# Expert stages on sorted rows: from two groups of batches with closed 128-row pieces to chunks whose pieces stay open

## The chip, the cores and the metric

The kernel runs on one core of one Trainium2 chip. The metric is the device time of one launch in microseconds (us). The engines are TensorE (PE; its weight loads are listed as PEld), VectorE (DVE), ScalarE (ACT), GpSimd (POOL) and SyncE (SP), which only issues transfers. Each has its own list of instructions, run in order; they meet through semaphores.

## The reference, cut to what matters

```python
x = x + attn_a(layernorm(x))      # linear attention, rope, elu+1 features, 16 heads of 8
x = x + ffn(layernorm(x))         # stage 1 of the experts
x = x + attn_b(layernorm(x))      # causal "log" attention with two score passes
x = x + ffn(layernorm(x))         # stage 2, the same weights

def ffn(x):                       # x is (8*512, 128); I = 256, E = 8, TOP_K = 2
    shared = silu(x @ sg_w.T) * (x @ su_w.T) @ sd_w.T
    probs = sigmoid(x @ router_w.T + routing_bias)
    topk_p, topk_idx = top_k(probs, 2); topk_p = topk_p / topk_p.sum(-1)
    # every row: two experts, each down(silu(gate x) * up x), weighted and added
    return shared + routed
```

There are 8 batches of 512 rows of 128 floats, so 4096 rows and 8192 pairs of a row and an expert.

## The kernel before, in words

All rows stay on the core (`x_res`, four tiles of 128 rows a batch). The four parts of the network run one after the other, each with its own program on each engine, and each part already does some work of the next one ("lead").

**Linear attention** goes batch by batch (`a_tensor_step`, `a_vector_step`, ...: steps 1 to 9, step 9 only ends batch 8).

**An expert stage** (class `Experts`) first normalises and transposes each batch and computes router logits. Then it *routes* a group of batches: a chain of small DVE instructions, each of which waits for the one before through `chain`, finds the two experts of each row (`vector_first`, `vector_second`), PE counts ranks (`tensor_ranks`), and DVE makes of them a row number in a list sorted by expert (`vector_place`, rows_of) and the expert of each 128-row slot (`vector_table`, table). POOL then *sends* every tile twice with an indirect DMA into `x_sorted` in DRAM (`send_tiles`, line 950; two per 128 rows), padded so that every expert's rows fill whole slots of 128. SP loads the slots four at a time (a *quad*, 1027), PE transposes them (743), and two slots make a *pair*: gate and up (`pair_gate_up`, 758, with the weights of the slot's expert), silu on ACT (863), the product on DVE (1204), a transpose (771), ACT's copy (871), down (`pair_down`, 781). ACT evicts and stores a quad to `y_sorted` (885, 890). When the quads of a group are stored, POOL *fetches* each batch's 8 tiles with indirect DMAs (960), and DVE adds them to `x_res` with their gates (`add_routed`, 1220). The *shared* expert is dense, batch by batch, and stands between pairs where the table `shared_after` says (724, 735, DVE 1195 and 1211).

Before, stage 1 has groups of 3 and 5 batches: 31 + 47 slots, 16 + 24 pairs. Stage 2 has 6 and 2: 55 + 23 slots, 28 + 12 pairs. Each group is padded by itself, so a stage is 40 pairs. Group 0 of stage 1 is routed and sent in step 7 of the linear attention; group 0 of stage 2 is routed during the last steps of the log attention (`lead_vector(k)`; k counts steps after the first score pass has ended) and sent from k = 13 on, three tiles a step, the rest behind it (`lead_pool`, `pool`). The group behind is routed while pairs of the first run. In the last 12 pairs of stage 1 the log attention's start stands in the slots of `TENSOR_LEAD`, `SCALAR_LEAD` and `VECTOR_LEAD` (projections of its first batch: q, ky, k).

**Log attention** (610 us): 80 steps of two score passes, B 16 steps behind A. POOL fetches the rows of stage 1's last batches during it, one tile a step (`late_fetch`).

## Time and profile before

| | us |
|---|---|
| median of 3 runs | 1392.99 (1386.32 to 1395.81) |
| the profiled execution | 1393.95 |
| its span | 1392.2 |
| mean granted TensorE clock | 0.831 |
| linear attention, to the first pair | 0 to 172.9 |
| stage 1 | 172.9 to about 449 |
| log attention, to the first pair of stage 2 | about 449 to 1129.8 |
| stage 2 | 1129.8 to 1392.2 |

The span runs from the first to the last instruction of one execution; 1.75 us of the profiled execution's time lie around it. The times at which parts begin and end are start times of their first and last matmuls, and neighbouring parts overlap on the other engines.

### The profile page before, as it was taken

What the parts mean: (1) busy time and instruction counts of PE and PEld (TensorE: products, weight loads), DVE (VectorE), ACT (ScalarE), POOL (GpSimd) and SP (SyncE); (2) the same over time, 40 slices, a digit from 0 to 9 for tenths busy, and PEclk for the clock granted to TensorE, in tenths of its full rate; (3) what the DMA queues carried; (4) which work ended last, traced back from release to release, by engine and by line L of the source; (5) the groups of instructions that cost most, each with busy time, mean ns of one, the idle gap of its engine ahead of it and who ended that gap; (6) DMA issues with size and microseconds to landing.
All of it is one profiled execution on the core that took longest, in us unless ns stands there. A gap on an engine that the chain in (4) does not pass through costs nothing.

```text
span 1392.2 us, 19740 instructions
## 1 busy us (share of the span) xinstructions
PE 957.8 (69%) x6976; PEld 569.3 (41%) x6976; DVE 657.1 (47%) x1314; ACT 607.2 (44%) x876; POOL 457.9 (33%) x527
## 2 busy tenths in 40 slices
PE   4776388528588766878787878786756078799241
PEld 3665256426355323333333333333333056566120
DVE  4787234202132345786777777775363033222022
ACT  1231063103145564777686877766422034254020
POOL 1113410640610343554433333342117600401734
PEclk9787589769889677999898999996587599999665
DMA  9400210121224344344443434311001211122222
GB/s 304 144 1 19 62 32 16 48 68 37 72 69 141 127 151 151 130 150 140 142 142 123 142 125 156 116 44 55 31 1 46 67 31 31 61 74 83 60 66 81
DMA packets 110557, 123.29 MB, mean 89 GB/s; under 512 B 9472, under 2 KB 72832, under 8 KB 110336
## 3 DMA queue, kind: packets, MB, share of 16 engines
q1 hardware_dynamic: 81664, 95.01, 20.9%
q0 software_dynamic: 8192, 16.79, 4.1%
q10 hardware_dynamic: 20608, 10.23, 2.5%
q8 instruction: 61, 1.00, 0.3%
q14 instruction: 32, 0.26, 0.1%
HBM read 60.52 MB, written 61.47 MB: 88 GB/s over the span
## 4 chain that ended last, share of the span: by engine, by line
PE 40%; DVE 16%; another core or an unknown queue 15%; issue 10%; DMA 9%; ACT 5%; SPq 4%; POOL 1%; DVEq 0%; POOLq 0%; ACTq 0%
PE psum L758 8%; DVE ring_b L1675 7%; PE psum L1470 5%; PE psum L1422 5%; PE psum L781 4%; DMA stacks<-stack_qr 4%; PE psum L724 2%; PE psum L771 2%; SPq L1820 2%; PE psum L735 2%; PE psum L1487 2%; DMA stacks<-stack_ky 2%; SPq L1815 2%; PE psum L743 1%
## 5 line engine op out<-in xcount | busy, mean ns | idle before, releaser
L1675 DVE TENSOR_SCALAR ring_b<-psum 128x1024 int32<-128x1024 int32 x160 | 195.7, 1223 | 129.0 <-PE psum L1422 128.8
L1549 ACT ACTIVATE ring_a<-psum 128x1024 f32<-128x1024 f32 x160 | 163.5, 1026 | 140.9 <-PE psum L1422 139.3
L1422 PE MATMUL psum<-stacks 32*128 32x128 f32 (+3 forms) x1024 | 107.1, 399 | 129.8 <-DVE ring_b L1675 97.2
L1555 ACT ACTIVATE ring_b<-ring_b 128x1024 f32<-128x1024 f32 x160 | 168.6, 1055 | 44.3 <-DVE ring_b L1675 44.3
L960 POOL DMA_INDIRECT r_rows<-y_sorted,rows_of x128 | 128.3, 1002 | 180.7 <-DMA y_sorted<-y_out 133.9
L758 PE MATMUL psum<-w_expert,ring_a 128*128 x312 | 160.8, 640 | 32.5 <-ACT ring_a L878 27.7
L950 POOL DMA_INDIRECT x_sorted<-r_rows,rows_of x128 | 124.1, 970 | 157.8 <-DVE rows_of L1170 120.5
L1781 POOL TENSOR_SCALAR_AFFINE_SELECT ring_b<-ring_b 128x512 f32<-128x512 f32 (+1 forms) x112 | 81.6, 741 | 284.5 <-ACT ring_b L1555 284.5
L1204 DVE TENSOR_TENSOR ring_b<-psum,ring_b 128x512 f32<-128x512 f32 x80 | 54.2, 677 | 223.9 <-ACT ring_b L863 184.9
L1422 PEld LDWEIGHTS psum<-stacks 32*128 32x128 f32 x1024 | 62.9, 201 | 225.0 <-ACT ring_a L1549 84.8
L1667 DVE TENSOR_SCALAR ring_a<-ring_a 128x1024 f32<-128x1024 f32 x160 | 122.7, 770 | 34.4 <-ACT ring_a L1549 34.4
L781 PE MATMUL psum<-w_expert,ring_b 128*128 x624 | 92.4, 295 | 47.2 <-DVE x_res L1211 24.6
L863 ACT ACTIVATE ring_b<-psum 128x512 f32<-128x512 f32 x80 | 47.0, 588 | 173.1 <-PE psum L758 106.8
L1470 PE MATMUL psum<-ring_b,values 128*32 128x256 f32 (+3 forms) x1024 | 111.7, 513 | 0.0
L1470 PE MATMUL psum<-ring_b,ones_s 128*32 128x256 f32 (+3 forms) x1024 | 110.1, 506 | 0.0
L1781 POOL TENSOR_SCALAR_AFFINE_SELECT ring_a<-ring_a 128x512 f32<-128x512 f32 (+1 forms) x112 | 83.7, 761 | 75.6 <-DVE ring_a L1667 75.6
L781 PEld LDWEIGHTS psum<-w_expert,ring_b 128*128 128x128 f32 x624 | 84.4, 210 | 49.1 <-issue 49.1
L1454 PE MATMUL psum<-ring_a,ones_s 128*32 128x256 f32 (+3 forms) x1024 | 93.9, 476 | 2.5 <-POOL ring_a L1781 1.7
L735 PE MATMUL psum<-w_expert,ring_b 128*128 128x128 f32 x256 | 37.9, 309 | 78.4 <-DVE ring_b L1195 60.9
L758 PEld LDWEIGHTS psum<-w_expert,ring_a 128*128 128x128 f32 x312 | 57.6, 205 | 78.0 <-issue 77.8
L735 PEld LDWEIGHTS psum<-w_expert,ring_b 128*128 128x128 f32 x256 | 34.7, 217 | 85.4 <-DVE ring_b L1195 66.5
L771 PEld LDWEIGHTS psum<-identity,ring_b 128*128 128x128 f32 x312 | 40.8, 148 | 68.0 <-issue 65.9
(175 smaller groups left out, 1291.5 us busy)
## 6 DMA issues: line engine op xcount, KB each, us to landing
ring_a<-x_sorted SPq DMA_DIRECT2D x36, 256.0 KB
y_sorted<-y_out ACTq DMA_DIRECT2D x36, 256.0 KB
stack_q<-parts SPq DMA_DIRECT2D x32, 256.0 KB
stack_ky<-parts SPq DMA_DIRECT2D x32, 256.0 KB
stacks<-stack_q SPq DMA_DIRECT2D x32, 256.0 KB
stacks<-stack_ky SPq DMA_DIRECT2D x32, 256.0 KB
stack_k<-parts SPq DMA_DIRECT2D x32, 256.0 KB
stacks<-stack_k SPq DMA_DIRECT2D x32, 256.0 KB
```

Source lines behind the costliest of these rows:

```text
L735: mm = nc.tensor.matmul(tiles(bank(4))[:, t, :], hidden[:, (k + c) % 8, t * 128:(t + 1) * 128], w["w_expert"][:, at:at + D], start=c == 0, ...
L758: mm = nc.tensor.matmul(bank(2 * (k % 2) + m), x_turned[:, n % 2, (i % 4) * 128:(i % 4 + 1) * 128], w["w_expert"][:, bass.ds(columns[m], 2 ...
L781: mm = nc.tensor.matmul(tiles(bank(4))[:, i % 4, :], hidden_turned[:, j % 2, at:at + 128], w["w_expert"][:, bass.ds(self.columns[j][m] + ( ...
L950: nc.gpsimd.indirect_dma_start(out=x_sorted[g][0:self.slots[g] * 128, :], out_offset=bass.IndirectOffsetOnAxis(ap=rows_of[:, n, at + t:at ...
L960: nc.gpsimd.indirect_dma_start(out=fetched[:, b % 4, n, t, :], out_offset=None, in_=y_sorted[self.group_of(b)][0:self.slots[self.group_of( ...
L1422: mm = nc.tensor.matmul(bank(2 * pair + j % 2)[:, column:column + width], keys[rows, s, kb * 128:(kb + 1) * 128], queries[rows, s, q0:q0 + ...
L1470: mm = nc.tensor.matmul(psum[32 * j:32 * j + 32, into, q0:q0 + width], weight, ring[:, m % RING, j, column:column + width], start=i == 0, ...
L1549: nc.scalar.activation(exps[:, n % RING, 2 * u:2 * u + 2, :], psum[:, first:first + 2, :], ACT.Exp, scale=SCALE).then_inc(self.exp, 1)
L1555: nc.scalar.activation(part, part, ACT.Ln, bias=1.0).then_inc(self.ln, 1)
L1667: nc.vector.tensor_scalar(part, part, CLIP_LO, CLIP_HI, ALU.max, ALU.min).then_inc(self.clip, 1)
L1675: nc.vector.tensor_scalar(ring[:, m % RING, HEADS_B[u][0]:HEADS_B[u][1] + 1, :].bitcast(I32), psum[:, first:first + 2, :].bitcast(I32), 0x ...
L1781: ins = nc.gpsimd.affine_select(out=part, in_=part, pattern=[[0, part.ap[1][1]], [1, 128]], compare_op=ALU.is_ge, fill=0.0, base=0, channe ...
```

## The change

The sorted list of a stage becomes one list of 71 pieces of 128 rows ("pages" in the code) that several *chunks* of batches fill: 4 and 4 in stage 1, and 3, 3 and 2 in stage 2. A chunk may end in the middle of an expert's piece; the next chunk of batches goes on there (`room_left`, `next_row`), and opens new pieces only behind the open ones. A stage is padded once, and is 36 pairs in 18 quads.

- Pieces that chunk 0 fills for certain come first: 6 quads (12 pairs) in stage 1 and 4 quads (8 pairs) in stage 2 (`quads_soon`). They need only chunk 0's sends (`sent_soon`). From there on a quad's load waits for the sends of all chunks, and its pair for the last chunk's table.
- The chain of a chunk is 49, 42 or 38 instructions (first, middle, last) in place of 26 and 5.
- Stage 1: chunk 0 (batches 1 to 4) is routed in steps 7 and 8 of the linear attention instead of 6 and 7. POOL sends 20 tiles, does `pool_rstd` of batch 5, and sends 12 more; the rstd of batches 6 to 8 stand behind that. Shared batches 1, 2 and 3 go ahead of the first pair, batches 7 and 8 behind pairs 29 and 31.
- Stage 2: chunk 0 is routed in lead steps 8 to 11 and sent from k = 11, chunk 1 in steps 12 to 16 and sent from k = 19 and behind it; the last chunk's rows stand behind pair 5. Shared batches 7 and 8 go behind pairs 29 and 33.
- Fetches of a chunk begin when the pieces that it can reach are stored: 10 quads for stage 1's chunk 0; 8 and 14 quads for stage 2's chunks 0 and 1. The last chunk of stage 1, fetched during log attention, is 32 tiles instead of 40.
- The lead of the log attention begins 9 pairs before the end of stage 1 and is 12 steps long, so that its last three steps (with k's projection) stand behind the last pair.

```diff
-SIZES_1, SIZES_2 = (3, 5), (6, 2)
-MOST = TT * max(*SIZES_1, *SIZES_2)
-
-
-def slots_of(batches):
+CHUNKS_1, CHUNKS_2 = (4, 4), (3, 3, 2)
+MOST = TT * max(*CHUNKS_1, *CHUNKS_2)
+
+
+def pages_of(batches):
     return (2 * batches * T + ROUTED * 127) // 128
 
...
                 ffn_1.vector_first(v, 0)
-            if b == 7:
+            if b == 8:
                 ffn_1.vector_gates(v, 0)
-                ffn_1.vector_place(v, 0)
+                ffn_1.vector_pages(v, 0)
+                ffn_1.vector_rows(v, 0)
...
-            ffn_1.send(p, 0)
+            ffn_1.send(p, 0, 0, 20)
+            ffn_1.pool_rstd(p, ffn_1.first_late)
+            ffn_1.send(p, 0, 20)
...
+                self.all_pairs, self.all_quads = (PAGES + 1) // 2, (PAGES + 3) // 4
+                self.early = B - chunks[-1]
+                self.first_late = self.early + 1
+                self.quads_soon = (2 * chunks[0] * TT - ROUTED + 1) // 4
+                self.offset = 0 if led else len(shared_first)
+                self.scored = B - self.first_late + 3
+                self.lead_from = self.all_pairs - 9
...
+                soon = n < self.quads_soon
+                if j == 0:
+                    pe.wait_ge(self.chain, self.chain_at(0, SOON_TABLE))
+                if n == self.quads_soon:
+                    pe.wait_ge(self.chain, self.chain_at(len(self.chunks) - 1, LINKS["last"]))
+                columns = [pe.value_load(table[0:1, 0 if soon else 1, i:i + 1], min_val=3 * INNER, max_val=ROUTED * 3 * INNER)
                            for i in slots]
...
+                else:
+                    for n, b in enumerate(self.shared_first):
+                        self.shared_gate_up(pe, b, 0)
+                        if n > 0:
+                            self.shared_down(pe, b - 1)
+                        self.shared_gate_up(pe, b, 1)
+                        self.late_tensor(pe, n)
+                    self.shared_down(pe, self.shared_first[-1])
...
+                for n in range(self.all_pairs - self.lead_from, LEAD_STEPS):
+                    if n in TENSOR_LEAD:
+                        self.following.tensor_step(pe, TENSOR_LEAD[n])
...
+
+                c = self.chunk_ending(b)
+                if b == 1:
+                    p.wait_ge(self.sent_soon, 16 * 2 * self.tiles(0))
+                    p.wait_ge(self.sent, 16 * 2 * (TT * B - self.tiles(0)))
+                if b == self.first_of(c):
+                    quads = self.quads_earlier + (pages_of(self.last_of(c)) + 3) // 4
                     for k in range(2):
                         p.wait_ge(y_stored[k], 16 * ((quads + 1 - k) // 2))
                 if b > 4:
...
+                if k == 15:
+                    self.pool_rstd(p, self.first_late)
+                if 11 <= k < 19:
+                    self.send(p, 0, 3 * (k - 11), 3 * (k - 10))
+                if 19 <= k:
+                    self.send(p, 1, 3 * (k - 19), 3 * (k - 18))
...
                 if self.led:
-                    self.send_tiles(p, 0, 3 * (11 - self.sizes[0]), 2 * self.tiles(0))
-                for b in range(self.first_late, B + 1):
+                    self.send(p, 1, 3 * (2 * DUS + 3 - 19))
+                for b in range(self.first_late + 1, B + 1):
                     self.pool_rstd(p, b)
-                self.send(p, 1)
...
+                    if n == 0:
+                        sp.wait_ge(self.sent_soon, 16 * 2 * self.tiles(0))
+                    if n == self.quads_soon:
+                        sp.wait_ge(self.sent, 16 * 2 * (TT * B - self.tiles(0)))
...
+                if k in (8, 12):
+                    self.vector_first(v, (8, 12).index(k))
+                if k in (8, 13):
+                    self.vector_second(v, (8, 13).index(k))
+                if k in (9, 14):
+                    self.vector_gates(v, (9, 14).index(k))
+                    self.vector_pages(v, (9, 14).index(k))
+                if k in (10, 15):
+                    self.vector_rows(v, (10, 15).index(k))
+                if k == 14:
+                    self.vector_stats(v, self.first_late)
+                if k in (11, 16):
+                    self.vector_experts(v, (11, 16).index(k))
                 if k - 17 in self.shared_first:
                     self.vector_shared(v, k - 17)
...
+                if n == self.scored:
+                    self.vector_first(v, last)
+                    self.vector_second(v, last)
+                if n == self.scored + 1:
+                    self.vector_gates(v, last)
+                    self.vector_pages(v, last)
+                    self.vector_rows(v, last)
+                if n == self.scored + 2:
+                    self.vector_experts(v, last)
...
-        ffn_1 = Experts("f1", AttentionDone(), SIZES_1, shared_first=(),
-                        shared_after={7: (1,), 9: (2, 3), 11: (4, 5), 13: (6, 7), 15: (8,)}, adds_after={22: (1,), 25: (2,), 27: (3,)})
+        ffn_1 = Experts("f1", AttentionDone(), CHUNKS_1, shared_first=(1, 2, 3),
+                        shared_after={3: (4,), 7: (5,), 9: (6,), 29: (7,), 31: (8,)}, adds_after={26: (1,), 29: (2,), 31: (3,), 34: (4,)})
         log_attn = LogAttention(ffn_1)
-        ffn_2 = Experts("f2", log_attn, SIZES_2, shared_first=(1, 2, 3),
-                        shared_after={1: (4,), 3: (5,), 5: (6,), 7: (7,), 9: (8,)}, adds_after={33: (1,), 36: (2,), 38: (3,)},
-                        led=True)
+        ffn_2 = Experts("f2", log_attn, CHUNKS_2, shared_first=(1, 2, 3),
+                        shared_after={1: (4,), 3: (5,), 5: (6,), 29: (7,), 33: (8,)},
+                        adds_after={23: (1,), 25: (2,), 28: (3,), 34: (4,)}, led=True)
         ffn_1.following, log_attn.following = log_attn, ffn_2
         stored = sem("stored")
...
```

POOL's list from the sends at the end of the linear attention to the memset behind stage 1's fetches. x_sorted is the sorted list in DRAM, f_rstd the layernorm factor of a later batch (L940, after: L980), L950 (L991) a send and L960 (L998) a fetch. Before:

```order
L950 DMA x_sorted<-r_rows,rows_of 3968x128 [waits x_zeroed,f1_chain]
L950 DMA x_sorted<-r_rows,rows_of 3968x128 x23
L940 TENSOR_TENSOR f_rstd<-f_var_eps,neg_half 128x4 [waits f1_var_ready] x5
L950 DMA x_sorted<-r_rows,rows_of 6016x128 [waits x_zeroed,f1_chain]
L950 DMA x_sorted<-r_rows,rows_of 6016x128 x39
L960 DMA r_rows<-y_sorted,rows_of 128x128 [waits y_stored1,y_stored0,f1_sent]
L960 DMA r_rows<-y_sorted,rows_of 128x128 x23
L1009 MEMSET values 128x4096 [waits a_sum]
```

After:

```order
L991 DMA x_sorted<-r_rows,rows_of 9088x128 [waits x_zeroed,f1_chain]
L991 DMA x_sorted<-r_rows,rows_of 9088x128 x19
L980 TENSOR_TENSOR f_rstd<-f_var_eps,neg_half 128x4 [waits f1_var_ready]
L991 DMA x_sorted<-r_rows,rows_of 9088x128 x12
L980 TENSOR_TENSOR f_rstd<-f_var_eps,neg_half 128x4 [waits f1_var_ready] x3
L991 DMA x_sorted<-r_rows,rows_of 9088x128 [waits f1_chain]
L991 DMA x_sorted<-r_rows,rows_of 9088x128 x31
L998 DMA r_rows<-y_sorted,rows_of 128x128 [waits y_stored0,y_stored1,f1_sent,f1_sent_soon]
L998 DMA r_rows<-y_sorted,rows_of 128x128 x31
L1054 MEMSET values 128x4096 [waits a_sum]
```

The first run of sends is 32 long instead of 24 and holds one f_rstd inside; the other three f_rstd stand behind it; the second run is 32 instead of 40 and the fetches are 32 instead of 24.

PE's list behind the last matmul of the linear attention (L258). Before, a quad's transpose (L743) and the first pair come next:

```order
L258 MATMUL psum<-w_a,oT 128x128 x4
L743 MATMUL psum<-identity,ring_a 128x128 x4
L751 TENSOR_LOAD table
L751 ISA x2
L751 TENSOR_LOAD table
L751 ISA x2
L758 ISA
L758 MATMUL psum<-w_expert,ring_a 128x512
```

After, three shared batches (L731 gate and up, L742 down) with the transposes (L688) and logits (L699) of late batches between them come first, and then the quad (L750):

```order
L258 MATMUL psum<-w_a,oT 128x128 x4
L731 MATMUL psum<-stacks,w_shared 128x512 x18
L742 MATMUL psum<-w_expert,ring_b 128x128 x8
L731 MATMUL psum<-stacks,w_shared 128x512 x6
L688 MATMUL psum<-identity,r_rows 128x128 x4
L731 MATMUL psum<-stacks,w_shared 128x512 x6
L742 MATMUL psum<-w_expert,ring_b 128x128 x8
L731 MATMUL psum<-stacks,w_shared 128x512 x6
L699 MATMUL psum<-w_router,xT 128x8 x4
L688 MATMUL psum<-identity,r_rows 128x128 x4
L742 MATMUL psum<-w_expert,ring_b 128x128 x8
L750 MATMUL psum<-identity,ring_a 128x128 x4
```

What moved: the shared work of batches 1 to 3 and two transposes of late batches, from between the pairs to ahead of the first one.

POOL's list at the end of the log attention, with the masks of its last steps (AFFINE_SELECT). Before, the sends of group 0 go on behind the last mask, and group 1's stand behind two f_rstd:

```order
L950 DMA x_sorted<-r_rows,rows_of 7040x128 [waits x_zeroed,f2_chain]
L950 DMA x_sorted<-r_rows,rows_of 7040x128 x2
L1781 AFFINE_SELECT ring_b<-ring_b 128x4x128 [waits b_ln]
L950 DMA x_sorted<-r_rows,rows_of 7040x128 x3
L1781 AFFINE_SELECT ring_b<-ring_b 128x4x128 [waits b_ln]
L1781 AFFINE_SELECT ring_b<-ring_b 128x4x128
L950 DMA x_sorted<-r_rows,rows_of 7040x128 x3
L1781 AFFINE_SELECT ring_b<-ring_b 128x4x128 [waits b_ln]
L950 DMA x_sorted<-r_rows,rows_of 7040x128 x39
L940 TENSOR_TENSOR f_rstd<-f_var_eps,neg_half 128x4 [waits f2_var_ready] x2
L950 DMA x_sorted<-r_rows,rows_of 2944x128 [waits x_zeroed,f2_chain]
L950 DMA x_sorted<-r_rows,rows_of 2944x128 x15
```

After (nine sends of chunk 0 stand ahead of this piece, and the x9 is its last), chunk 1's 24 follow behind the last mask:

```order
L991 DMA x_sorted<-r_rows,rows_of 9088x128 x3
L1935 AFFINE_SELECT ring_b<-ring_b 128x4x128 [waits b_ln]
L1935 AFFINE_SELECT ring_b<-ring_b 128x4x128
L980 TENSOR_TENSOR f_rstd<-f_var_eps,neg_half 128x4 [waits f2_var_ready]
L991 DMA x_sorted<-r_rows,rows_of 9088x128 x3
L1935 AFFINE_SELECT ring_b<-ring_b 128x4x128 [waits b_ln]
L991 DMA x_sorted<-r_rows,rows_of 9088x128 x9
L991 DMA x_sorted<-r_rows,rows_of 9088x128 [waits f2_chain]
L991 DMA x_sorted<-r_rows,rows_of 9088x128 x23
L980 TENSOR_TENSOR f_rstd<-f_var_eps,neg_half 128x4 [waits f2_var_ready]
L991 DMA x_sorted<-r_rows,rows_of 9088x128 [waits f2_chain]
L991 DMA x_sorted<-r_rows,rows_of 9088x128 x15
```

The run behind the last mask is 33 sends instead of 39, and the 16 sends of the last chunk stay behind an f_rstd.

## Rows read from the trace of the kernel before

**Rows 1.** Page: engine totals (busy us, share); then shares of the ending chain by engine.

```profile
PE 957.8 (69%) x6976; PEld 569.3 (41%) x6976; DVE 657.1 (47%) x1314; ACT 607.2 (44%) x876; POOL 457.9 (33%) x527
...
PE 40%; DVE 16%; another core or an unknown queue 15%; issue 10%; DMA 9%; ACT 5%; SPq 4%; POOL 1%; DVEq 0%; POOLq 0%; ACTq 0%
```

**Rows 2.** Timeline, PE, two gate/up groups (start us, us, engine line op).

```profile
1222.48 1.88 PE L758 MATMUL psum<-w_expert,ring_a 128*128 x4
...
1261.58 1.88 PE L758 MATMUL psum<-w_expert,ring_a 128*128 x4
```

**Rows 3.** Timeline, PE, a shared batch and the pair behind it.

```profile
235.42 3.05 PE L724 MATMUL psum<-stacks,w_shared 128*128 128x512 f32 x12
...
241.77 1.88 PE L758 MATMUL psum<-w_expert,ring_a 128*128 x4
```

**Rows 4.** Timeline, first and last of 40 sends, ACT behind them; then windows.

```profile
250.59 1.03 POOL L950 DMA_INDIRECT x_sorted<-r_rows,rows_of  x1 [50.97 <-DVE rows_of L1170]
...
300.00 0.96 POOL L950 DMA_INDIRECT x_sorted<-r_rows,rows_of  x1 [0.30 <-issue]
...
307.10 0.60 ACT L863 ACTIVATE ring_b<-psum 128x512 f32<-128x512 f32 x1 [30.30 <-remote]
```

```profile
450.00:1060.00 610.00, 464.06 (x4439) 207.75 (x4443) 404.81 (x631) 392.63 (x482) 229.38 (x286) 0.85 0.33 112
...
258.00:307.00 49.00, 10.66 (x52) 8.51 (x52) 2.08 (x3) 1.20 (x2) 32.65 (x34) 0.67 0.19 63
```

**Rows 5.** Timeline, first and last of the 24 sends in linear attention, and after.

```profile
125.81 1.36 POOL L950 DMA_INDIRECT x_sorted<-r_rows,rows_of  x1 [14.61 <-DVE rows_of L1170]
...
155.37 0.96 POOL L950 DMA_INDIRECT x_sorted<-r_rows,rows_of  x1 [0.30 <-issue]
...
160.13 0.69 DVE L328 TENSOR_TENSOR x_res<-psum,x_res 128x512 f32<-128x512 f32 x1 [14.15 <-remote]
...
172.90 3.78 PE L758 MATMUL psum<-w_expert,ring_a 128*128 x4 [0.76 <-ACT ring_a L878]
```

**Rows 6.** Timeline, first of 24 fetches in stage 1, and ACT behind them.

```profile
352.74 0.99 POOL L960 DMA_INDIRECT r_rows<-y_sorted,rows_of  x1 [51.78 <-DMA y_sorted<-y_out]
...
386.77 0.59 ACT L878 COPY ring_a<-psum 128x512 f32<-128x512 f32 x1 [10.02 <-remote]
```

**Rows 7.** Timeline, end of log attention: last send run, ACT, first pair.

```profile
1059.24 0.98 POOL L950 DMA_INDIRECT x_sorted<-r_rows,rows_of  x1 [0.17 <-issue]
...
1107.75 0.96 POOL L950 DMA_INDIRECT x_sorted<-r_rows,rows_of  x1 [0.31 <-issue]
...
1114.27 1.09 ACT L855 ACTIVATE ring_b<-psum 128x512 f32<-128x512 f32 x2 [40.12 <-remote]
...
1129.84 1.98 PE L758 MATMUL psum<-w_expert,ring_a 128*128 x4 [0.85 <-ACT ring_a L878]
```

**Rows 8.** Timeline, first and last of 16 sends in stage 2.

```profile
1189.34 1.03 POOL L950 DMA_INDIRECT x_sorted<-r_rows,rows_of  x1 [53.09 <-DVE rows_of L1170]
...
1208.39 0.96 POOL L950 DMA_INDIRECT x_sorted<-r_rows,rows_of  x1 [0.30 <-issue]
```

**Rows 9.** Timeline, pair 12 of stage 2; first of 48 fetches; ACT behind 40.

```profile
1215.85 1.98 PE L758 MATMUL psum<-w_expert,ring_a 128*128 x4 [0.75 <-issue]
...
1279.85 0.99 POOL L960 DMA_INDIRECT r_rows<-y_sorted,rows_of  x1 [70.50 <-DMA y_sorted<-y_out]
...
1336.26 0.59 ACT L878 COPY ring_a<-psum 128x512 f32<-128x512 f32 x1 [20.45 <-remote]
```

**Rows 10.** Timeline, SP and PE where stage 1 hands over to log attention.

```profile
437.86 2.45 SPq L1815 DMA_DIRECT2D stack_ky<-parts  x4
...
457.72 0.80 PE L1422 MATMUL psum<-stacks 32*128 32x512 f32 x4 [8.97 <-DMA stacks<-stack_ky]
```

**Rows 11.** Timeline, DVE: one routing instruction on 96 columns, one on 192.

```profile
105.41 0.26 DVE L1102 TENSOR_TENSOR ring_a<-ring_a,choice_rank 128x96 f32<-128x96 f32 x1
...
1024.03 0.36 DVE L1121 TENSOR_TENSOR ring_a<-ring_a,choice_rank 128x192 f32<-128x192 f32 x1
```

617 lines of the change are left out of this document (345 added, 272 removed).

## The prediction

> **What bounds the kernel now.** I read the engine totals and the chain's shares first. PE is busy 69% and leads the chain with 40%, but 15% of the chain goes to "another core or an unknown queue" [rows 1], and there is no other core. So I looked in the timeline at where the engines stand still with that releaser. It is always the same picture: POOL issues indirect DMAs one behind another, and some 8 us later PE, DVE and ACT nearly stop, until about 6 us after the last. The clearest one is the second send run of stage 1: first send at 250.59, last at 300.00 (40 sends, 1.264 us apart), ACT goes on at 307.10 after 30.30 us of waiting, and from 258 to 307 PE was busy for 10.66 of 49 us [rows 4]. In the trace ACT and DVE wait there for signals of matmuls that by their rows had ended long before. The same stands behind the 24 sends in the linear attention (125.81 to 155.37, DVE on at 160.13) [rows 5], the 24 fetches of stage 1 (from 352.74, ACT on at 386.77) [rows 6], the sends at the end of the log attention (1059.24 to 1107.75, ACT on at 1114.27 after 40.12 us) [rows 7] and the first 40 fetches of stage 2 (from 1279.85, ACT on at 1336.26) [rows 9]. In the log attention, where POOL issues one fetch a step, PE is busy 464 of 610 us [rows 4]: single indirect DMAs don't do it. What delays the signals the trace doesn't say; I take the size from the rows.
>
> Between such runs an expert stage is bound by PE. Twelve pairs took 1261.58 - 1222.48 = 39.1 us, 3.26 each [rows 2]; a shared batch takes 241.77 - 235.42 = 6.35 us [rows 3].
>
> So the time of a stage is work (pairs, shared batches, late batches) plus the length of the runs of indirect DMAs, less some 8 us of free time and a trickle in each.
>
> **The change, part by part.** The sum is made against the profiled execution, 1393.95 us, which is 1 us over the median; the 1.75 us around the span stay.
>
> 1. *Pairs.* 40 - 36 = 4 fewer a stage, on the bounding engine: 4 x 3.26 = 13.0 us off each, 26.1 in all. Their quads (20 to 18) are inside the 3.26.
>
> 2. *Stage 1, first run.* Before, 24 sends start at 125.81, right behind the row numbers, and the first pair starts at 172.90 [rows 5]. Now chunk 0 has four batches: its ranks and rows stand one step of the linear attention later (steps are 14 to 17 us), with 19 small instructions instead of 8; one on 96 columns takes 0.26 us, one on 192 takes 0.36 [rows 11]. So sends start at about 144 (bounds 138 and 148). 32 of them, with one f_rstd inside, take 40.5 + 1 us, to about 185, and PE's signals come freely again at about 190. The linear attention's last step falls into this run as it does today, so "attention done" moves from 172.9 to about 190: +17. The late batches' f_rstd (6 to 8) stand behind the run on POOL, and DVE's bias of batch 6 waits for it ahead of shared batch 2's product; I cost that at nothing, because the run's standstill covers it until about 188; without that cover it costs up to two shared batches' time, 12.7 us. The three shared batches ahead of the first pair are only moved. In the longer standstill a little more gets done (PE did 22% of its time in the one above): -3. One late batch fewer (four instead of five): -2. Net with the pairs: 17 - 3 - 2 - 13 = -1.
>
> 3. *Stage 1, the other two runs.* Sends 40 to 32: -8 x 1.264 = -10.1. Fetches 24 to 32: +10.1. Net 0. PE has 7 pairs and 2 shared batches of allowed work (about 36 us) beside the second run, against 41 + 6 us; since a run lets only 8 us plus a trickle through, that work isn't used up, and I expect no wait of its own for pair 12's rows.
>
> 4. *Hand-over to the log attention.* Today ky's store is issued at 437.86, some 11 us before the last pair ends, and its first full scores wait until 457.72 for the stack's loads [rows 10], 20 us behind. Now ky's low part is DVE's slot 8, which is the last pair, and k's projection stands behind all pairs. The same 20 us then begin 3 to 4 us before the last pair ends: +8 (bounds 0, if the pairs gone by leave SP's queue free, and +12).
>
> 5. *The log attention itself* has 8 fetches fewer among its steps, which are hidden: 0 (bounds -3 and 0). At its end DVE routes two chunks: 49 + 42 + 6 instructions against 26 + 5 + 1, so 65 more, at 0.26 to 0.29 us instead of 0.36: about 13 us more DVE time in the B-only steps. Some of it goes where DVE waits for PE; I take +8 for when the run behind the last mask starts, and that run has 33 sends instead of 39: -7.6. Three shared batches, the last output and the first pair follow it as today (1114.27 to 1129.84 [rows 7]). With chunk 0 sent three tiles a step and one step's earlier start, I take -3 for the first pair (bounds -10 and +8).
>
> 6. *Stage 2, the wait at pair 8.* Today pair 12 starts at 1215.85, 86 us behind pair 0, with all shared batches done [rows 7, 9]. Now pairs 8 and on need the last chunk's 16 sends. These start behind pair 5, which today's pace puts 43 us behind pair 0 with its routing (7 links more), run 20 us (today's from 1189.34 to 1208.39 [rows 8]), and the load and transpose take 4 to 6: pair 8 about 74 us behind pair 0. Work worth 8 x 3.26 + 3 x 6.35 + 6 (two late batches) = 51 is done in them, so 23 us are lost, where today 86 - (12 x 3.26 + 5 x 6.35 + 6) = 9 are lost: +14 (bounds +5 and +21).
>
> 7. *Stage 2, fetches.* 48 and 16 become 24, 24 and 16. The last 16 and the adds behind the last pair are as today. The other 48 tiles are two runs of 30 us with about 8 free us each instead of one of 40 and one of 8: two standstills of about 20 lost us against 42: -2.
>
> Sum: -1 + 0 + 8 - 3 + (14 - 13) - 2 = +3. 1393.95 + 3 = 1397, and 1396 on the median's scale.
>
> **A rule against this reading.** [Rows 4] show matmul signals standing still beside a run of indirect DMAs, with DVE busy 2.08 of 49 us. The Trainium skill, page "SBUF — State Buffer", section "SBUF: two separate sides", says that transfers and compute use disjoint ports and that a DMA cannot be slowed by a compute op nor the other way round; its one exception is GpSimd held off by DVE, and POOL's issue here kept its 1.264 us throughout. The rule would give the first rival below; the trace disagrees with it as far as a standstill of 30 us can be anything but a coincidence, but no row names the cause.
>
> **The rivals.**
>
> *The standstills don't follow the run's length.* If they hang on something of today's schedule (which matmuls and quads meet the sends), the moved sends may miss it, and the 8 pairs count in full: 1394 - 26 = 1368; with half of the standstill terms kept, 1380. For it: the free 8 us vary, and shorter runs (24, 24, 16) could lie wholly beside pairs. Against it: five runs of 24 to 40, in four different surroundings, show the same. Chance of over 1% faster: 0.29.
>
> *The longer chain of small DVE instructions is on the path.* It is at home in the last 9 steps of the log attention and in the last chunk of stage 2. Over the kernel there are about 100 more routing instructions, 27 us at 0.27. My sum holds about 12 of it. If B's score passes wait for each of them, the sends behind the last mask start 14 us later instead of 8, and pair 8's wait grows to its bound: 6 + 7, and with the hand-over's bound of 4 more: 1396 + 17 = 1413. It decides if that run of 33 starts later than about 1072 (today's 39 at 1059.24). For it: in steps 10 to 12 today the score passes do stand behind routing. Against it: DVE has gaps of 6 us there. Chance of over 1% slower: 0.25.
>
> *The change doesn't pay off because work is only moved:* that is my forecast, 0.46.
>
> **How the numbers follow.** The forecast is 1396. A change under 1% (14 us) can't be told from none by this measurement. The known terms are small against the unknown ones: items 2, 4, 5 and 6 have bounds of -9 to +17, -8 to +4, -7 to +11 and -9 to +7 around what I took (item 2 with the cover gone and the start at its bounds). Taken together that is some 15 us to each side; with the two rivals, 1368 to 1418 leaves out about 2 in 10: the whole gain of the pairs with still shorter standstills below it, and a second mishap in stage 1 above it. Chances: 0.29 faster, 0.46 within 1%, 0.25 slower.
>
> **What would show it.** In the changed profile: 36 pairs a stage at 3.26 us where POOL is quiet; the first send near 144, the first pair near 212, with standstills in three runs of 32; first full scores 15 to 20 us behind stage 1's last pair; a run of 33 sends ending near 1105; pair 8 of stage 2 some 74 us behind pair 0 with PE waiting for a quad. I am wrong if the linear attention ends while sends still run and shared batches go on at full pace beside them (then the first rival), or if the log attention ends over 10 us later than its start moved (then the second).

## The result, and the profile of the changed kernel

The changed kernel takes 1407.08 us (median of 4 runs, 1401.13 to 1412.19) against 1390.47 us of the kernel before (4 runs, 1386.32 to 1395.81): a ratio of 1.0133, with a 95% interval of 1.0094 to 1.0172. It is slower by 1.3%, just over the 1% that this measurement can tell from nothing. The forecast was 1396 within 1368 to 1418, so the time lies in the range, 11 us above the forecast, and on the slower side, to which the prediction gave 0.25. How much of that is luck is said further down. The profiled execution took 1412.19 us (span 1410.4), 5 us over its median; before it was 1393.95, so the two traces differ by 18.2 us, where the prediction's sum said 3.

The page of the changed kernel, engine totals and the shares of the ending chain (they answer to [rows 1]):

```profile
PE 935.5 (66%) x6851; PEld 556.1 (39%) x6851; DVE 674.2 (48%) x1408; ACT 595.3 (42%) x853; POOL 456.6 (32%) x527
...
PE 40%; DVE 17%; issue 11%; another core or an unknown queue 11%; DMA 9%; ACT 4%; SPq 4%; POOL 2%; DVEq 0%; POOLq 0%; ACTq 0%
```

PE has 22.3 us less to do, DVE 17.1 us more in 94 more instructions, and the span is longer. What has to be read is therefore where the engines wait. The timeline of stage 1, POOL's first and last sends of each run and PE behind them (start us, us, engine line op, idle time before and what ended it; they answer to [rows 4, 5]):

```profile
142.93 1.36 POOL L991 DMA_INDIRECT x_sorted<-r_rows,rows_of  x1 [28.34 <-DVE rows_of L1261]
...
170.75 2.90 PE L731 MATMUL psum<-stacks,w_shared 128*128 128x512 f32 x6 [8.71 <-issue]
...
183.98 0.95 POOL L991 DMA_INDIRECT x_sorted<-r_rows,rows_of  x1 [0.30 <-issue]
...
186.94 2.90 PE L731 MATMUL psum<-stacks,w_shared 128*128 128x512 f32 x6 [9.26 <-DVE ring_b L1318]
...
200.13 1.98 PE L768 MATMUL psum<-w_expert,ring_a 128*128 x4 [0.95 <-ACT ring_a L908]
...
243.03 1.03 POOL L991 DMA_INDIRECT x_sorted<-r_rows,rows_of  x1 [42.35 <-DVE rows_of L1261]
...
282.29 0.96 POOL L991 DMA_INDIRECT x_sorted<-r_rows,rows_of  x1 [0.30 <-issue]
...
290.26 3.75 PE L742 MATMUL psum<-w_expert,ring_b 128*128 128x128 f32 x16 [28.59 <-DVE ring_b L1318]
```

The first send stands at 142.93 and the first pair at 200.13. Beside this first run PE doesn't stand still in the way that the prediction took. The linear attention ends at 158.6, while sends are still going out (before: at 172.0), and PE then waits 8.71 and 9.26 us in the shared batches. Each of these waits ends right behind a DVE instruction (L1093, the bias of a late batch) that had waited 11.23 and 13.44 us for POOL's f_rstd, and the f_rstd (168.75 and 184.95) stand behind 20 and behind all 32 sends in POOL's order. The second run has 32 sends, and beside this one PE does stop: it waits 28.59 us for a product whose own matmuls had long ended, until 8 us behind the last send. The group with which it goes on takes 3.75 us, where the same one takes 2.05 when PE has been busy: the granted clock had fallen to 0.50 (the 1.2 GHz level) during the stop, as the first row of the next table shows (windows: length, busy time of PE, weight loads, DVE, ACT, POOL, granted clock, DMA share, GB/s).

```profile
258.00:279.00 21.00, 2.93 (x6) 1.84 (x6) 0.69 (x1) 1.17 (x2) 15.85 (x17) 0.50 0.16 53
1132.15:1217.01 84.86, 46.04 (x226) 34.06 (x226) 22.79 (x68) 21.98 (x40) 16.46 (x17) 0.79 0.09 27
1217.01:1410.40 193.39, 115.70 (x583) 80.41 (x583) 41.66 (x99) 51.17 (x93) 60.64 (x64) 0.79 0.24 70
```

The other two rows are stage 2 from pair 0's first group to the first group behind the wait for the last chunk's rows, and from there to the end. That group (1217.01) is pair 7's: PE transposes the quad of pairs 8 and 9 ahead of it, and it is the eighth gate/up group of the stage. The fetches of stage 1 (answering to [rows 6]), the hand-over to the log attention (to [rows 10]) and the end of the log attention with stage 2's first pair (to [rows 7]):

```profile
354.39 0.98 POOL L998 DMA_INDIRECT r_rows<-y_sorted,rows_of  x1 [71.15 <-DMA y_sorted<-y_out]
...
400.29 2.07 PE L768 MATMUL psum<-w_expert,ring_a 128*128 x2 [22.41 <-ACT ring_a L908]
...
465.30 0.80 PE L1574 MATMUL psum<-stacks 32*128 32x512 f32 x4 [17.94 <-DMA stacks<-stack_ky]
...
1069.10 0.97 POOL L991 DMA_INDIRECT x_sorted<-r_rows,rows_of  x1 [0.17 <-issue]
...
1109.60 0.96 POOL L991 DMA_INDIRECT x_sorted<-r_rows,rows_of  x1 [0.30 <-issue]
...
1132.15 1.98 PE L768 MATMUL psum<-w_expert,ring_a 128*128 x4 [0.85 <-ACT ring_a L908]
```

Then stage 2 around that wait, with pair 7 (1217.01), pair 8 (1222.73) and the first fetch (to [rows 8, 9]):

```profile
1190.92 0.17 DVE L1261 CAST rows_of<-ring_a 128x16 int32<-128x16 f32 x1
...
1191.39 1.03 POOL L991 DMA_INDIRECT x_sorted<-r_rows,rows_of  x1 [52.80 <-DVE rows_of L1261]
...
1215.47 1.11 PE L750 MATMUL psum<-identity,ring_a 128*128 128x128 f32 x4 [25.97 <-DMA ring_a<-x_sorted]
1217.01 3.78 PE L768 MATMUL psum<-w_expert,ring_a 128*128 x4 [0.42 <-issue]
...
1222.73 1.88 PE L768 MATMUL psum<-w_expert,ring_a 128*128 x4
...
1264.21 1.00 POOL L998 DMA_INDIRECT r_rows<-y_sorted,rows_of  x1 [52.83 <-DMA y_sorted<-y_out]
...
1298.24 2.07 PE L768 MATMUL psum<-w_expert,ring_a 128*128 x2 [20.27 <-ACT ring_a L908]
```

The 18.2 us in three steps. The log attention's first full scores come at 465.30 instead of 457.72: +7.6 for stage 1 and the hand-over. From there to stage 2's first pair the changed kernel is 5.3 us quicker (666.9 us against 672.1). Stage 2 from its first pair to the end takes 278.3 us instead of 262.4: +15.9, although it has four pairs (13 us) less. PE stands still for 25.97 us at the transposition of the quad of pairs 8 and 9, where it waits for the rows of the last chunk, and for 20.27, 7.62 and 12.13 us beside the fetches.

### The profile page after: what moved, and what is told of

Its sections match the earlier page's. It is cut to its first block, busy times and chain, and to the rows that moved or that the text cites. A ratio compares the mean times of both kernels' runs of the same rounds, so it can differ in the third digit from the quotient of the medians.

```text
span 1410.4 us, 19431 instructions
## 1 busy us (share of the span) xinstructions
PE 935.5 (66%) x6851; PEld 556.1 (39%) x6851; DVE 674.2 (48%) x1408; ACT 595.3 (42%) x853; POOL 456.6 (32%) x527
## 4 chain that ended last, share of the span: by engine, by line
PE 40%; DVE 17%; issue 11%; another core or an unknown queue 11%; DMA 9%; ACT 4%; SPq 4%; POOL 2%; DVEq 0%; POOLq 0%; ACTq 0%
PE psum L768 8%; DVE ring_b L1829 7%; PE psum L1622 5%; PE psum L1574 5%; PE psum L791 4%; DMA stacks<-stack_qr 3%; PE psum L731 2%; SPq L1974 2%; PE psum L742 2%; PE psum L781 2%; SPq L1969 2%; DMA stacks<-stack_ky 2%; PE psum L1639 2%; DMA stack_q<-parts 1%
## 5 line engine op out<-in xcount | busy, mean ns | idle before, releaser
L998 POOL DMA_INDIRECT r_rows<-y_sorted,rows_of x128 | 126.8, 991 | 215.1 <-DMA y_sorted<-y_out 164.0
L768 PE MATMUL psum<-w_expert,ring_a 128*128 x284 | 145.5, 637 | 48.2 <-ACT ring_a L908 44.5
L991 POOL DMA_INDIRECT x_sorted<-r_rows,rows_of x128 | 124.1, 970 | 160.8 <-DVE rows_of L1261 123.8
L1327 DVE TENSOR_TENSOR ring_b<-psum,ring_b 128x512 f32<-128x512 f32 x72 | 49.2, 683 | 243.7 <-ACT ring_b L893 216.5
L893 ACT ACTIVATE ring_b<-psum 128x512 f32<-128x512 f32 x72 | 42.6, 591 | 139.3 <-PE psum L768 116.0
L742 PE MATMUL psum<-w_expert,ring_b 128*128 128x128 f32 x256 | 40.9, 325 | 86.4 <-DVE ring_b L1318 52.0
L791 PE MATMUL psum<-w_expert,ring_b 128*128 x568 | 82.2, 291 | 16.9 <-DVE x_res L1332 12.1
L768 PEld LDWEIGHTS psum<-w_expert,ring_a 128*128 128x128 f32 x284 | 52.0, 204 | 88.6 <-issue 88.6
L791 PEld LDWEIGHTS psum<-w_expert,ring_b 128*128 128x128 f32 x568 | 75.5, 207 | 18.4 <-issue 18.4
L742 PEld LDWEIGHTS psum<-w_expert,ring_b 128*128 128x128 f32 x256 | 37.8, 233 | 93.4 <-DVE ring_b L1318 57.9
L908 ACT COPY ring_a<-psum 128x512 f32<-128x512 f32 (+1 forms) x36 | 20.9, 580 | 109.1 <-PE psum L750 57.1
```

The source lines that it names most:

```text
L742: mm = nc.tensor.matmul(tiles(bank(4))[:, t, :], hidden[:, (k + c) % 8, t * 128:(t + 1) * 128], w["w_expert"][:, at:at + D], start=c == 0, ...
L768: mm = nc.tensor.matmul(bank(2 * (k % 2) + m), x_turned[:, n % 2, (i % 4) * 128:(i % 4 + 1) * 128], w["w_expert"][:, bass.ds(columns[m], 2 ...
L791: mm = nc.tensor.matmul(tiles(bank(4))[:, i % 4, :], hidden_turned[:, j % 2, at:at + 128], w["w_expert"][:, bass.ds(self.columns[j][m] + ( ...
L991: nc.gpsimd.indirect_dma_start(out=x_sorted, out_offset=bass.IndirectOffsetOnAxis(ap=rows_of[:, n, at + t:at + t + 1], axis=0), in_=x_rows ...
L998: nc.gpsimd.indirect_dma_start(out=fetched[:, b % 4, n, t, :], out_offset=None, in_=y_sorted[0:pages_of(self.last_of(self.chunk_ending(b)) ...
```

## Experiments

All ran against the kernel before on the same chip. The comparisons fell on four chips: in the first two the kernel before took 1388.83 and 1385.72 us, in the last two 1291.50 and 1293.24. That difference became a finding of its own; until then ratios are compared only among the first eight rows, where the changed kernel's 1.0133 belongs too (the kernel before took 1390.47 us beside it).

| run | kernel before, us | this, us | ratio (95%) |
|---|---|---|---|
| e5_half_sends | 1388.83 | 1388.42 | 0.9989 (0.9966 to 1.0011) |
| e1_shared_back | 1388.83 | 1408.61 | 1.0149 (1.0114 to 1.0183) |
| e2_rows_first | 1388.83 | 1404.89 | 1.0101 (1.0072 to 1.0130) |
| e7_gated | 1388.83 | 1364.80 | 0.9825 (0.9789 to 0.9862) |
| e3_handover | 1385.72 | 1400.80 | 1.0112 (1.0084 to 1.0140) |
| e6_plain_sends | 1385.72 | 1371.15 | 0.9896 (0.9861 to 0.9930) |
| e8_all_gated | 1385.72 | 1327.95 | 0.9583 (0.9554 to 0.9611) |
| e9_before_gated | 1385.72 | 1357.40 | 0.9812 (0.9779 to 0.9845) |
| e10_cover | 1291.50 | 1304.84 | 1.0100 (1.0071 to 1.0129) |
| e12_two_chunks | 1291.50 | 1347.91 | 1.0428 (1.0402 to 1.0455) |
| e11_combined | 1291.50 | 1261.71 | 0.9770 (0.9736 to 0.9804) |
| e13_combined_again | 1293.24 | 1264.70 | 0.9784 (0.9768 to 0.9801) |

### Does the stop follow the run's length?

The second half of stage 1's second run is left out, so this probe computes stage 1 on missing rows (`gt` is the chunk's 16 tiles; the waits on `sent` count 16 less):

```diff
                 gt, at = self.tiles(c), self.own(c).start
+                if c == 1 and not self.led:
+                    last = gt
```

> A probe of the standstill in stage 1's second run: the 16 sends of the second choices of batches 5 to 8 are left out, so rows of those choices are missing from the sorted rows (stage 1 computes on zeros there); the run has 16 sends instead of 32. Run-length theory (the standstill lasts from 8 us after the first send to 6 us after the last): PE goes on near 270 instead of 290, total 16 x 1.264 = 20 us shorter, about 1387, 0.998 of before. The prediction's first rival (standstills hang on something else than the run's length): less than 5 us, 1402 to 1407.

The ratio is 0.9989 against 1.0133: 1.44% or 20.0 us less, as the run's length said. PE waits 6.01 us at the place where it waited 28.59, and goes on 6.3 us behind the last send (262.11); the row is from the timeline of this probe:

```profile
268.44 3.78 PE L742 MATMUL psum<-w_expert,ring_b 128*128 128x128 f32 x16 [6.01 <-DVE ring_b L1320]
```

### Is it the transfers, or the indirect form?

```diff
+                    if c == 1 and not self.led:
+                        nc.gpsimd.dma_start(x_sorted[(40 + k) * 128 - 128:(40 + k) * 128, :],
+                                            x_rows[:, (at + t) // TT, t % TT, :]).then_inc(self.sent, 16)
+                        continue
                     nc.gpsimd.indirect_dma_start(
```

> A probe of what in the runs holds PE's signals up: the 32 indirect sends of stage 1's second run are replaced by 32 plain DMAs of the same tiles from the same POOL queue, to fixed rows (rows of batches 5 to 8 are left unsorted, so stage 1 computes on wrong rows there). If the standstill comes from transfers from POOL's queue as such: plain DMAs at about the same pace give the same stop, 28 us idle before pair 10, total 1407 or less by what the issue is shorter. If it comes from the indirect form (the addresses made on POOL): no stop, PE goes on through pairs 8 to 11, total 25 to 35 us shorter, about 1377, 0.99 of before.

The ratio is 0.9896, 1371 us. The timeline of POOL in this probe, and the window from 243 to 290 of this probe:

```profile
244.22 17.08 POOL L992 DMA_DIRECT2D x_sorted<-r_rows  x32 [41.85 <-DVE rows_of L1265]
```

```profile
243.00:290.00 47.00, 44.18 (x242) 31.41 (x241) 14.10 (x25) 19.56 (x35) 17.08 (x32) 0.99 0.35 107
```

The same window in the changed kernel, where the 32 sends are indirect:

```profile
243.00:290.00 47.00, 13.38 (x63) 8.97 (x61) 5.35 (x11) 6.17 (x11) 30.76 (x32) 0.64 0.23 73
```

The plain transfers take POOL 0.53 us each (17.08 / 32) instead of 1.264 from issue to issue, they move the same 64 KB each, and PE is busy for 44.18 of 47 us instead of 13.38. Transfers from POOL's queue as such stop nothing; back-to-back indirect ones do. One caution: a run of 17 us is also shorter than one of 40, but by the length alone a stop of some 15 us would be left (17 less 8 and 6 more), and none is seen. It isn't the chip either. In e3_handover, which ran beside this probe on the same chip with the 32 indirect sends (242.47 to 281.74), the stop is there:

```profile
288.85 3.78 PE L742 MATMUL psum<-w_expert,ring_b 128*128 128x128 f32 x16 [30.05 <-DVE ring_b L1318]
```

### Is it the number of indirect DMAs, or that they come without a gap?

The fetches are gated in threes, each three behind the product of the next pair. This is the core of it; POOL's first f_rstd for the log attention moves ahead of the twelfth fetch, and some adds one to two pairs later:

```diff
+                        f = (b - 1) * 2 * TT + n * TT + t
+                        j = 20 + f // 3 if self.led else 0 if f < 8 else 27 + (f - 8) // 3
+                        if f == 11 and self.following.takes_rest:
+                            self.following.pool_step(p, -12)
+                        if 0 < j < self.all_pairs:
+                            p.wait_ge(self.hidden, self.items.index(("pair", j)) + 1)
                         self.fetch_tile(p, b, n, t)
```

> POOL's fetches in both stages go in threes, each three behind a wait for the product of the next pair (from the ninth fetch on in stage 1, from the first in stage 2), and the adds and the log attention's first f_rstd are moved to fit. If only long back-to-back runs hold the signals up (as the threes in the log attention's end suggest): pairs go on at about 3.8 us beside the threes, the idle 30 us in stage 1 and 40 us in stage 2 shrink to 6 to 10 each, total -30 to -45, about 1370, 0.985 of before. If each DMA holds the signals up however it is spaced: every pair there takes 8 us or more, total the same or up to 40 us slower, 1407 to 1447.

The ratio is 0.9825, 42 us less than the changed kernel, with every DMA still there. Windows over the fetches of stage 1 and of stage 2, of this run:

```profile
352.50:415.00 62.50, 52.02 (x270) 35.45 (x268) 22.02 (x62) 23.66 (x44) 31.48 (x33) 0.97 0.29 78
1231.00:1352.00 121.00, 67.83 (x331) 46.94 (x329) 29.79 (x77) 27.68 (x51) 60.93 (x64) 0.81 0.28 77
```

and of the changed kernel:

```profile
354.00:417.00 63.00, 28.91 (x135) 20.28 (x134) 9.80 (x27) 12.84 (x24) 34.93 (x34) 0.73 0.17 49
1264.00:1401.00 137.00, 68.71 (x346) 48.66 (x344) 30.39 (x78) 29.11 (x53) 60.00 (x64) 0.76 0.23 67
```

In stage 1 PE does 52.02 us of work in the 62.5 us in which it did 28.91 before, and the granted clock is 0.97 instead of 0.73. In stage 2 the same 64 fetches and the same PE work fit into 121 us instead of 137. So on this chip the number doesn't cost, the missing gap does.

The gates don't make threes in the trace, though. Where POOL comes late, several gates are already open. The fetches of stage 1 go out in runs of 8, 3, 6, 6, 3 and 6, those of stage 2 in runs of 9, 6, 9, 18, 6 and 16. Beside stage 1's the longest wait of PE is 2.28 us; in stage 2 waits of 4.43 and 5.25 us are left, and one of 9.74 us beside the run of 18.

The sends get the same treatment in the next run: stage 1's second run, and the 24 sends of chunk 1 at the end of the log attention.

```diff
+                    if c == 1 and k % 3 == 0:
+                        if self.led:
+                            p.wait_ge(self.hidden, min(k // 3 + 1, 7) if k < 21 else 8)
+                            if k == 18:
+                                self.pool_rstd(p, B)
+                        elif k >= 6:
+                            p.wait_ge(self.hidden, self.items.index(("pair", 4)) + k // 3)
```

> The kernel with the fetches in threes, and two of the send runs in threes too: stage 1's second run (from its seventh send on, each three behind the next product) and the 24 sends of chunk 1 at the end of the log attention (each three behind the next product of the shared batches and pair 0). If threes are harmless for sends as for fetches: the 28.6 us of idle time at 290 shrink to under 10 with pair 12's rows there at about 293 (-11 to -20), and pair 0 of stage 2 starts some 20 us sooner (-15 to -25); total 1365 minus 26 to 45, about 1330, 0.957 of before. Rival (what waits for the rows then is late by what the gaps add, so the stop only changes its name): within 8 us of 1365.

The ratio is 0.9583: 1328 us as expected, 5.4% under the changed kernel. The window of stage 1's second run of sends, of this run:

```profile
243.00:290.00 47.00, 30.75 (x147) 22.07 (x146) 10.04 (x18) 10.51 (x20) 28.92 (x31) 0.82 0.17 55
```

PE is busy for 30.75 of the 47 us instead of 13.38. The 32 sends go out in runs of 15, 9 and 8 there. Beside the 15 and just behind them PE still waits 4.40 and 5.95 us for products, and at the end 4.82 us for the rows themselves.

### Does the kernel before gain the same?

The same gate on the fetches of the kernel before (from pair 23 in stage 1, from pair 32 in stage 2, from the ninth fetch on):

```diff
+                        j = 0 if f < 8 else (32 if self.led else 23) + (f - 8) // 3
```

> The kernel before (not the changed one) with the same gate on its fetches: from the ninth on in threes, each behind the next pair's product, in both stages. If the standstill is a property of the runs and not of the changed chunks: stage 1 gains about 18 us, stage 2 (POOL then bounds it, 64 x 1.264 from 1279.85) about 20, total 1390 - 38 = 1352, 0.973, which would put it ahead of the changed kernel with its gate (1365). If the changed kernel's three chunks are what lets fetches hide: less than half of it, 1375 or more.

The ratio is 0.9812, 26 us gained (28 by the medians), less than the 38 expected and more than the half of it that the other theory allowed. Windows over the fetches of both stages, of this run, and then of the kernel before:

```profile
352.00:400.00 48.00, 43.94 (x225) 29.32 (x224) 17.36 (x54) 23.14 (x43) 20.94 (x19) 0.96 0.29 80
1253.00:1347.00 94.00, 33.61 (x155) 22.18 (x154) 23.79 (x73) 14.13 (x27) 60.58 (x64) 0.65 0.31 83
```

```profile
352.70:400.00 47.30, 27.77 (x120) 18.74 (x119) 8.84 (x23) 11.03 (x20) 26.43 (x25) 0.75 0.25 68
1280.00:1392.00 112.00, 35.87 (x152) 24.41 (x150) 23.16 (x73) 13.99 (x26) 60.42 (x64) 0.64 0.26 70
```

With gated fetches the two kernels are level (0.9812 and 0.9825). The changed kernel gains 42 us by the gate and the kernel before 26; the 16 us between them are what the change had lost on balance. A reason can be read from the traces, but no run tests it alone. In the kernel before, stage 2's fetches start some 8 pairs from the end, so that 64 of them are POOL's own 81 us whatever PE does; with three chunks they start 16 pairs from the end, and there is work to lay beside them.

### The wait at pair 8

First, shared batches 7 and 8 of stage 2 moved forward, and alone, shared batch 6 moved back behind the routing:

```diff
-                        shared_after={1: (4,), 3: (5,), 5: (6,), 29: (7,), 33: (8,)},
+                        shared_after={1: (4,), 3: (5,), 5: (6,), 7: (7, 8)},     # e1_shared_back
+                        shared_after={1: (4,), 3: (5,), 7: (6,), 29: (7,), 33: (8,)},     # e2_rows_first
```

> Shared batches 7 and 8 of stage 2 stand behind pair 7, ahead of the wait at pair 8, instead of behind pairs 29 and 33. Theory (the wait at pair 8 is uncovered, 34 us lost in it): pair 8 stays some 85 us behind pair 0, the stretch behind it is 2 x 6.35 = 12.7 us shorter, total about 1407 - 12.7 = 1394, 1.004 of the kernel before. Rival (the two batches are free where they stand, because PE stands still for 40 us beside the fetches there anyway): total stays at 1407, 1.013.

> Only shared batch 6 of stage 2 moves from behind pair 5 to behind pair 7, so that on DVE the last chunk's gates, pages and rows no longer stand behind its products. Theory (the last 16 sends start late because of the order on DVE): first of the 16 sends 53 us behind pair 0 instead of 59, pair 8 at 79 us instead of 85, total -6, 1401, 1.009 of before. Rival (the routing's own waits, for the ranks on PE and for ACT's exponential, set the start): less than 2 us, total 1405 to 1407.

e1 came out at 1.0149, no gain. Its timeline shows that it wasn't the test I meant:

```profile
1202.92 1.11 PE L750 MATMUL psum<-identity,ring_a 128*128 128x128 f32 x4 [25.93 <-DMA ring_a<-x_sorted]
1204.44 3.77 PE L768 MATMUL psum<-w_expert,ring_a 128*128 x4 [0.41 <-issue]
...
1209.78 3.05 PE L731 MATMUL psum<-stacks,w_shared 128*128 128x512 f32 x12
```

PE waits in the transposition of the quad that holds pairs 8 and 9, and that stands in pair 6's place in PE's order, not in pair 8's; the group at 1204.44 is pair 7's. Work put behind pair 7 is behind the wait. What the run does show: batches 7 and 8 cost the same 12.7 us wherever they stand behind the wait. e2 came out at 1.0101; its sends start 72.9 us behind the last of the 33 (1106.91 to 1179.78) instead of 81.8, 8.9 us sooner, of which 6.35 us go to batch 6 that is now behind the wait. The ratio is 0.3% lower than the changed kernel's, with intervals that overlap.

Then the edit that the timeline asks for: DVE takes the last chunk's routing ahead of the shared batches, and batches 6, 7 and 8 stand behind pair 5.

```diff
-                        shared_after={1: (4,), 3: (5,), 5: (6,), 29: (7,), 33: (8,)},
+                        shared_after={1: (4,), 3: (5,), 5: (6, 7, 8)},
...
+                    soon = self.led and n == self.scored + 1
+                    if soon:
+                        self.late_vector(v, n)
                     for b in self.shared_after.get(j, ()):
                         self.vector_shared(v, b)
                     self.late_logits(v, n)
-                    self.late_vector(v, n)
+                    if not soon:
+                        self.late_vector(v, n)
```

> The changed kernel, fetches and sends as they are, with two edits in stage 2: on DVE the last chunk's gates, pages and rows come directly behind pair 5's product, and shared batches 6, 7 and 8 all stand behind pair 5, which is ahead of the transposition at which PE waits (the run with batches 7 and 8 behind pair 7 had them behind it). Theory (that wait is uncovered and late): the 16 sends start 9 us sooner against the 33 sends' end, and the three batches go on for 8 us of the run; PE's wait at the transposition falls from 26 us to 8 to 15; total 1407 - 17 = 1390, 1.000 of the kernel before (1384 to 1396). Rival (the loss comes back in the fetch runs, as with batches 7 and 8 moved): 1403 or more.

The ratio is 1.0100, but the kernel before took 1291.50 us on this chip, so the numbers of the expectation can't be held against it; the changed kernel itself has no time there. The mechanism can be read. The wait at the transposition is 4.34 us (25.97 in the changed kernel on the first chip):

```profile
1156.46 1.11 PE L750 MATMUL psum<-identity,ring_a 128*128 128x128 f32 x4 [4.34 <-DMA ring_a<-x_sorted]
```

What else this trace shows is in the next part.

### A chip on which PE goes on

The second run of sends of stage 1 is untouched in e10_cover, 32 back-to-back indirect DMAs at the same 1.264 us. The same window, first of e10_cover:

```profile
243.00:282.00 39.00, 25.71 (x144) 18.79 (x142) 9.72 (x16) 10.61 (x19) 28.74 (x30) 0.90 0.20 66
```

and, of the changed kernel on the first chip:

```profile
243.00:282.00 39.00, 13.38 (x63) 8.97 (x61) 4.26 (x9) 5.09 (x9) 29.80 (x31) 0.67 0.20 64
```

PE gets 25.71 us of work done beside the same run instead of 13.38, and then waits 13.19 us for the rows (at 284.73), not for signals. The kernel before is 7% faster on this chip. The two traces differ beside the runs and not in general: from its first full scores to the same group of scores near its end the log attention takes 583 us here (437.64 to 1020.52) and 578 in the changed kernel (465.30 to 1043.73), and at the first send run of stage 1, where PE waits for f_rstd, the windows are close, first of e10_cover and then of the changed kernel:

```profile
141.00:200.00 59.00, 32.01 (x140) 26.07 (x140) 20.81 (x72) 13.21 (x26) 35.67 (x36) 0.71 0.18 58
141.00:200.00 59.00, 29.49 (x132) 24.36 (x132) 21.91 (x75) 12.67 (x25) 35.03 (x36) 0.66 0.17 54
```

But the chip alone doesn't decide it. Within this one execution PE stops beside the 32 fetches of stage 1 (a wait of 23.70 us) and goes on beside the first 24 fetches of stage 2, as these windows of e10_cover show:

```profile
333.00:378.00 45.00, 18.33 (x93) 12.60 (x90) 7.15 (x23) 8.99 (x17) 34.69 (x34) 0.76 0.27 69
1204.00:1240.00 36.00, 34.18 (x189) 23.45 (x188) 13.65 (x35) 17.46 (x32) 22.70 (x24) 1.00 0.45 123
```

Both are back-to-back indirect fetches at the same pace. So the stop depends on the chip or session on which a run falls, and on what else goes on beside it; nothing in the traces says on what. The changed kernel with the better cover is still 1.0% slower than the kernel before here, so the pairs taken away don't count in full on this chip either.

On the same chip I undid the third chunk: `CHUNKS_2 = (6, 2)`, still with pieces that stay open, with the routing of six batches in the steps 10 to 14 of the log attention's end, the sends from step 14 on, and shared batches 4 to 8 behind pairs 1 to 9.

> Stage 2 of the changed kernel with the chunks 6 + 2 of the kernel before, still in one set of 71 pages with pieces that stay open, 36 pairs, shared batches 4 to 8 behind pairs 1 to 9 as before; stage 1 as in the changed kernel. It undoes the third chunk alone. If my sum is right that the third chunk puts a wait at pair 8 that two chunks have not: no wait of over 5 us for rows, fetches in runs of 40 and 24; 1390.5 - 13 (pairs) - 2 + 8 (stage 1 and hand-over as measured) = 1383, 0.995 of before; 24 us under the changed kernel. Rival (stage 2 loses its pairs' gain through its fetches, which start later with long chunks, whichever the chunks): 1395 to 1407.

The ratio is 1.0428, 43 us slower than e10_cover beside it. Two waits that e10_cover doesn't have are in its timeline and window:

```profile
1105.72 1.08 PE L757 MATMUL psum<-identity,ring_a 128*128 128x128 f32 x4 [29.79 <-DMA ring_a<-x_sorted]
```

```profile
1263.00:1349.00 86.00, 18.17 (x81) 12.57 (x79) 20.70 (x69) 7.39 (x14) 60.66 (x64) 0.59 0.32 85
```

Pair 0 needs all 48 sends of the six batches, 42 of which run at the end, and waits 29.79 us for them; and the fetches start so late that 64 stand in one row behind nearly all pairs, with PE busy for 18.17 of 86 us. My expectation (0.995) had taken neither into account. It is not a clean undoing: the routing's steps were set anew, and e10_cover has the order and the cover of the last chunk besides. The kernel before has two chunks too and takes 1291.50 us on this chip, 13 us less than e10_cover. So this says only that two chunks with this placing are slow; what the third chunk is worth by itself isn't shown.

### The hand-over

```diff
-        SCALAR_LEAD = {1: -11, 2: -10, 4: -7, 6: -6, 8: -5, 10: -4, 11: -1}
-        VECTOR_LEAD = {0: -12, 5: -3, 6: -6, 8: -5, 9: -2, 10: -4}
-        TENSOR_LEAD = {3: -8, 5: -7, 7: -6, 9: -5}
+        SCALAR_LEAD = {0: -11, 1: -10, 2: -7, 4: -6, 6: -5, 8: -4, 9: -1}
+        VECTOR_LEAD = {0: -12, 3: -3, 4: -6, 6: -5, 7: -2, 8: -4}
+        TENSOR_LEAD = {2: -8, 3: -7, 5: -6, 7: -5}
```

> The changed kernel with the log attention's lead slots in stage 1 moved up so that ky's low part is DVE's slot 6 (pair 33) instead of slot 8 (pair 35), and k's projection stands before the last pair. Theory (the hand-over lost 7.6 us because these slots shrank from 12 pairs to 9): first full scores start 6 us sooner behind the stage's last pair, total 1407 - 6 = 1401, 1.009 of the kernel before. Rival (the 18 us wait for the stack is SP's queue, not the slot): no change, 1407.

The timeline of this run, the last pair's last matmul and the first full scores:

```profile
443.87 0.71 PE L791 MATMUL psum<-w_expert,ring_b 128*128 x4 [0.55 <-ACT ring_b L901]
...
458.31 0.80 PE L1574 MATMUL psum<-stacks 32*128 32x512 f32 x4 [13.73 <-DMA stacks<-stack_ky]
```

They are 14.4 us apart, against 19.5 (445.79 to 465.30) in the changed kernel: 5.1 us sooner, where 6 were expected. The ratio, 1.0112 against 1.0133, goes that way, but its interval doesn't exclude nothing.

### All together

The gates on fetches and sends (the last chunk's too, from the seventh on), the edit of e10_cover, the slots of e3_handover, and batch 4's fetches of stage 1 left to the log attention's steps.

> All together on the changed kernel: the gates on fetches and on sends (with the last chunk's 16 sends gated too, from the seventh on), stage 2's routing and shared batches 6 to 8 ahead of the wait, the hand-over's slots moved up, and batch 4's fetches of stage 1 left to the log attention's steps. Against the run with all gates (1328): stage 2's wait of 26 us shrinks to under 8 (-18), hand-over -4, eight fetches fewer beside stage 1's last pairs -3; 1303, 0.940 of before. If POOL's pace, not PE, bounds stage 2's end once the sends are gated: only -8 in all, 1320.

> The combined kernel once more, because the kernel before took 1291.5 us in the last comparison and 1386 to 1389 in the ones before it, so that its 0.977 can't be set against the 0.958 of the run with all gates. If the kernel before is at 1386 to 1391 again (PE nearly stopped beside long runs of sends): the wait at stage 2's transposition is under 8 us instead of 26.0, the first full scores of the log attention 4 us sooner behind the pairs, total 1328 - 18 - 4 - 3 = 1303, 0.940; if the moved batches give the time back as they did without gates, 1320 or more, 0.952 or more. If the kernel before is at 1291 again: 0.977 again, and the standstill goes with the chip that a run falls on.

Both runs fell on chips on which the kernel before takes 1292: 0.9770 and 0.9784, that is 1262 and 1265 us, 2.2% faster than the kernel before, and 3.3% faster than e10_cover on the same chip (1261.71 against 1304.84). The 0.940 expected of e11_combined was missed, and the third case written down for e13_combined_again came: 0.977 again. The gates do little on these chips: in e11_combined the second send run of stage 1 still goes out as 32 back to back and the fetches of stage 2 as 24 and 40, because PE keeps ahead of POOL. The wait ahead of pair 8 in the second of them:

```profile
1117.98 1.11 PE L751 MATMUL psum<-identity,ring_a 128*128 128x128 f32 x4 [3.98 <-DMA ring_a<-x_sorted]
```

The changed kernel waits 25.97 us there on the first chip. It has no trace on this one, so how much of the difference is the cover isn't shown. What the combination gives on a chip on which PE stops wasn't measured; there the version with all gates has 0.9583.

## Why the prediction was right or wrong

By its own steps, with the measured value behind each.

**What bounds the kernel.** Right for the second send run and for the fetches on the chips of the first two comparisons: a stage is work plus the runs' length, less some 8 us. Half the run took off 20.0 us (20 expected); all gates took 5.4% off. It didn't hold for the first send run of the changed kernel on the same chip, nor for all runs on the other chips.

**Item 1, pairs.** They still take 3.26 us each. The 13 us a stage are gone and went into waits.

**Items 2 and 3, stage 1.** Here the number is right by luck. The first send was at 142.93 (144 said) and the first pair at 200.13 (212 said). Item 2 had the linear attention's last step stopped beside the sends, so that it ends 17 us later, and put POOL's f_rstd behind them at nothing. In the trace it ends 13 us sooner (158.6 against 172.0), since the later run no longer meets its steps, and what PE then waits for, 8.71 and 9.26 us, is the f_rstd in the send run's shadow; e10_cover has the same two waits, 9.21 and 8.14 us, on its chip. So the first pair came 12 us too soon for the sum. Behind it item 3 was too low by about as much: from the first pair to the last pair's last matmul it is 245.7 us, where the sum has some 235. PE's waits beside the second run are 33.9 us against 39.3 before (-5.4, -10.1 said), beside the fetches 32.2 against 19.5 (+12.7, +10.1 said), and it waits 4.64 us instead of 1.08 for the chosen experts ahead of the ranks. The two errors cancel: the last pair's end came 2 to 3 us sooner than before, -1 said.

**Item 4, hand-over.** First full scores at 465.30, +7.6; the sum had -1 + 8 = +7. e3_handover shows the slots as its cause, for 5 of it.

**Item 5, end of the log attention.** -5.3 us (-3 said), the 33 sends ending at 1109.60 (1105 said).

**Item 6, the wait at pair 8. This is the step that failed most,** as a size. It said that pair 8 comes 74 us behind pair 0 and that this costs +14 (bounds 5 and 21). It came 90.6 us behind (1222.73): 39 us over the 51 of work, where the kernel before lost 9, so +30, beyond the bound. I had let the sends start behind pair 5 with the routing, at about 43 us, and even so the terms as printed (43, 20 for the run, 4 to 6 for load and transpose) add up to 67 to 69, not to 74. In the trace they start at 1191.39, 59.2 us behind pair 0, since DVE's rows (1190.92) stand behind shared batch 6's products in its order, and since pairs 4 and 5, shared batch 6 and the ranks ran after short waits that the routing itself put there (PE waits 4.43 us for the chosen experts before the ranks). The rows are there at 1215.47, and pair 7, which stands behind the transposition, then takes 5.7 us instead of 3.26, because PE leaves the wait with its clock down: its first group takes 3.78 us where pair 12 took 1.98 [rows 9]. e2_rows_first shows 8.9 us of the late start as the place of shared batch 6 alone; e10_cover and e13_combined_again have 4.34 and 3.98 us of the wait left once that order and the cover of three shared batches are right, but both ran where sends hardly stop PE; how much of the cover would get through beside them on the other chips wasn't tried. I also spoke of a wait "at pair 8", and it stands in pair 6's place in PE's order; that error cost the first experiment its point.

**Item 7, fetches.** Right. Pair 8 to the end took 187.7 us. The kernel before took 176.35 for as many pairs [rows 9], and the two shared batches behind it add 12.7, so -1.4 where -2 was said. The stops themselves are as sized: 20.27 us beside the first run and 7.62 + 12.13 beside the second, 40 in all, against 6.59 + 13.72 + 18.24 + 5.72 = 44 in the kernel before. Some of that is given back at the end: from the first of the last 16 fetches (1381.93) to the end it is 28.5 us instead of 26.3.

Item 6 is off by 16 us, item 7 by 1, items 2 to 5 by -2, together the 15 us between the sum of 3 and the 18.2 of the traces.

**The rivals.** *The standstills don't follow the run's length:* refuted for the second send run and the fetches on those chips by e5_half_sends, e7_gated and e8_all_gated. It holds in part elsewhere. On the first chip itself the moved first run of 32 no longer met the linear attention's steps, half of the sign that I had written down for this rival; the shared batches then didn't go on at full pace, but for f_rstd. On two other chips the same runs stop PE less. The changed kernel by itself wasn't run there; e10_cover, which has less to wait for, was 1.0% slower than the kernel before. *The longer chain of small DVE instructions is on the path:* by its own test it wasn't. The run of 33 began at 1069.10, before 1072, and the log attention's end took less time, not more. The time is on its side for another reason, the order on DVE ahead of the last chunk's rows. *Work is only moved,* the forecast: with the fetches gated the two kernels are level, 0.9825 and 0.9812; without the gates the moved work costs 1.3%, outside the 1% to which the forecast gave 0.46.

**The rule.** The row is e6_plain_sends: 32 plain transfers of 64 KB beside PE at 44.18 of 47 us. There the trace agrees with the Trainium skill, page "SBUF — State Buffer", section "SBUF: two separate sides", which has transfers and compute on disjoint ports. Beside 32 indirect ones PE did 13.38 us in the same window of the changed kernel. No row shows that the ports are the cause, but by the rule alone nothing would have been slowed, so there the measurement decides, and the sum was right to go by the rows.

## What to carry to other kernels

When engines stand still with no releaser in the profile, look at what one queue issues back to back, and put gaps into that before you restructure the work: the gate is six lines and was worth 3% where the stops are, the pairs taken away were worth nothing. Look into the trace whether the gaps are really there: a gate on work that is already done lets the next transfers out back to back. Ask too what small instruction of the same queue stands behind the transfers; POOL's f_rstd behind the sends cost PE two waits of 9 us. Give each wait its place in each engine's order before you name what covers it; the transposition that waited stood two pairs ahead of the pair that it served. When a chunk is made smaller so that it can start sooner, what decides is the place of its last small instruction behind other work on the same engine.

## What the runs showed of the hardware that I had not expected

- Back-to-back indirect DMAs on POOL (1.264 us apart) went with waits of PE for products of matmuls that had ended, up to 28.59 us in the changed kernel and 30.05 us in e3_handover; broken into runs of 3 to 8 beside stage 1's fetches (e7_gated), the longest wait left was 2.28 us, and beside a run of 18 in the same trace it was 9.74 us.
- Plain DMAs of the same 64 KB from the same queue go out every 0.53 us, and PE was busy 94% of the time beside them.
- The effect isn't the same on every chip, nor beside every run: beside the same 32 sends PE was busy for 13.38 or for 25.71 of 39 us, within e10_cover for 18.33 of 45 us beside the fetches of stage 1 and for 34.18 of 36 us beside those of stage 2, and the kernel before took 1386 to 1391 us on some chips and 1292 on two others. Its cause stays open.
